# Mamba block and four expert layers on one core: the residual and the norm of a chunk moved from VectorE to TensorE and ScalarE, and both ends of the expert stage put in another order

## The chip, the cores and the metric

The kernel runs on one core of a Trainium2 chip. The metric is the time of one execution on the device, in microseconds (us). A core has five engines with queues of their own: TensorE (PE; its weight loads are shown as PEld), VectorE (DVE), ScalarE (ACT), GpSimd (POOL) and SyncE (SP), which here only issues DMAs.

## The reference

Input x has 4 sequences of 1024 tokens with 128 features. First comes a selective scan block, with 256 inner channels and 64 states each:

```
xn = layernorm(x); xi, z = split(xn @ W_in)
u = silu(causal_conv4(xi) + conv_b);  dt_r, Bm, Cm = split(u @ W_xproj)
delta = softplus(dt_r @ W_dt + b_dt)
h_t = h_{t-1} * exp(delta_t * A) + (delta_t * u_t) * B_t;  y_t = sum_n h_t * C_t
out = ((y + u * D) * silu(z)) @ W_out
x1 = layernorm(x + (x + out))
```

So the scan block's result is `2 x + out`, normalized (mean and variance, no weights). Then come 4 expert layers: a router picks 2 of 4 experts for each token, each expert normalizes its input, multiplies by w1 (128 x 512), takes the gelu and multiplies by w2 (512 x 128); the layer gives the weighted sum of `x + y_e`. The end is `layernorm(x1 + layers(x1))`.

## The kernel before, in words

**Front.** Eight items of 512 tokens are projected, convolved and split in bfloat16 parts, which go through DRAM. This part isn't changed.

**Scan stage.** Tokens are taken in chunks: 64 steps of a pair of sequences, 128 rows in all, 32 chunks (`NCH`). A chunk is two blocks of 128 channels (`kk` 0 and 1), a block eight quarters `q`; quarters 0 to 3 and 4 to 7 make its two groups. `run_blocks` runs `emit(c, pair, kk, last)` over all blocks on every engine, and the numbers `Q_...` say in which quarter an engine does a step for an older chunk. In a quarter

- TensorE computes products for B (`products`, L1180), a part of the sum over states (`sum_states`, L1197) and the arguments of exp for two quarters on (`arguments`, L1167);
- ScalarE computes the exponential for the next scan (`exponent`, L951) and copies products out of PSUM (`take_products`, L961);
- VectorE does one scan instruction of 128 x 1040 (L1519). The first scan of a group waits for all four copies of its group (`evac_done`).

A chunk's output follows two chunks later: ScalarE evacuates y (`evacuate`, L972), TensorE turns it and adds `u * D` (`turn`, L1209, L1211), VectorE gates it (`gate`, L1473), TensorE projects it (`project`, L1219), in block 0, quarter 3. Then VectorE adds the residual (`add_residual`, L1481: `2 x + projection`, into `xres`), takes the statistics (`chunk_stats`, `chunk_aggregate`, L1487, L1493) in quarters 4 to 6 of block 0, GpSimd computes `(var + eps) ** -0.5` (`chunk_rsqrt`, L697, L699), and VectorE writes the normalized rows to `x1c` in quarter 2 of block 1 (`chunk_norm`, L1368). ScalarE's queue stores them. SP loads x's rows, u and silu(z) of the next chunk (`load_post`) once that norm is done.

**Expert stage.** `run_layers` runs `step` for 4 layers x 8 groups of 512 tokens (`n` counts groups through all layers). In a step TensorE does for each expert `first` (L1294, 12 products) and `second` (L1306, 16), in the order first 0, first 1, second 0, transposes of the next group (`stage_xh`, L1273), first 2, second 1, first 3, second 2, second 3. ScalarE does the gelus (L1062, four an expert) and, ahead of expert 2 (in the first step ahead of expert 1, and again ahead of 2), centring and scaling for a group two on (`stage_norm`, L1037, L1043). VectorE has `stage_moments` for the group two on, `start_sum` (L1661), `add_expert` 0 to 3 (L1671), `split_xh` (L1679, L1681: the transposed tile in two parts), `stage_scores` (L1605 on), `stage_router` (L1617 to L1644), `sum_bias` (L1651, L1654). GpSimd computes the router's products (`stage_scores`, L826), the exponential (`stage_exp`, L818), the weighted biases (`stage_bias`, L835) and each `rsqrt` (L688). In the last layer VectorE also finishes the group before (`finish`: `X + X1` L1697, moments L1355 to L1363, scaling L1584), and SP stores it. `begin` holds what an engine does between the last scan and the first step.

A wait is a number that a semaphore has to reach; each engine works through its queue in order. The order is written by hand.

## Time and profile before

| | |
|---|---|
| median of 3 runs | 2242.97 us (2242.24 to 2248.36) |
| the profiled execution | 2246.93 us |
| its span, first to last instruction | 2245.1 us |
| TensorE busy | 2130.0 us (95%) |
| VectorE busy | 1838.6 us (82%) |
| ScalarE busy | 1596.8 us (71%) |
| GpSimd busy | 920.4 us (41%) |
| mean granted TensorE clock | 0.98 of full speed |

Times in the rows are us from the span's start. A row of the timeline has the start, the length, the engine, the line of the kernel, the operation, its output and inputs, and how many instructions were merged in it (x4); in brackets how long the engine had been idle before it, and whose work ended the idle time. Lengths of neighbours overlap: an instruction can start before the one ahead has ended. Scans run from 171.4 to 1355 us, the expert stage from there to the end.

### The profile page before, as it was taken

To read this page: it belongs to the slowest core of one execution; us is meant where nothing else is said; L and a number is where in the kernel's file an instruction comes from. 1 tells how busy PE (TensorE), PEld (TensorE's weight loads), DVE (VectorE), ACT (ScalarE), POOL (GpSimd) and SP (SyncE) were. 2 spreads that over 40 slices of the span, in tenths; PEclk is the share of its full clock that TensorE was granted. 3 is DMA by queue.
4 is the path that set the end of the run, shared out by engine and by line. 5 is a ranking of instruction groups with operands and counts; after the bars stand their busy time and mean duration, and the time that the engine had idled before them with its cause. 6 is when DMAs were issued, how large, how long until landed. Compare 5 with 4: busy or idle time off the path is not lost. (4 is left out here: it accounts for less than half of the span.)

```text
span 2245.1 us, 50361 instructions
## 1 busy us (share of the span) xinstructions
PE 2130.0 (95%) x16960; PEld 1258.0 (56%) x16960; DVE 1838.6 (82%) x2779; ACT 1596.8 (71%) x2070; POOL 920.4 (41%) x452
## 2 busy tenths in 40 slices
PE   7968999999999999999999997999999999999997
PEld 3432333333333333333333335999999999999986
DVE  6869999999999999999999996566555566556665
ACT  5868888888888888888888883545455455445543
POOL 3123334343443444343434344444444444444442
PEclk9977999999999999999999998999999999999999
DMA  5995222222222121212121234000100010000000
GB/s 171 279 281 136 43 46 45 42 46 41 45 42 46 41 46 40 46 40 46 40 46 40 47 96 135 1 0 0 38 1 0 0 39 1 0 1 1 10 11 18
DMA packets 354957, 114.93 MB, mean 51 GB/s; under 512 B 283000, under 2 KB 345600, under 8 KB 354624
## 3 DMA queue, kind: packets, MB, share of 16 engines
q1 hardware_dynamic: 350416, 110.92, 20.2%
q10 hardware_dynamic: 4464, 3.02, 0.4%
...
## 5 line engine op out<-in xcount | busy, mean ns | idle before, releaser
L1519 DVE TENSOR_TENSOR_SCAN arena<-behind 128x1040 f32<-128x1040 f32 x512 | 1157.0, 2309 | 21.1 <-ACT behind L961 18.2
L1062 ACT ACTIVATE arena<-PS,arena 128x512 f32<-128x512 f32 x512 | 342.9, 688 | 399.5 <-PE PS L1294 398.9
L951 ACT ACTIVATE behind<-PS 128x1024 f32<-128x1024 f32 x512 | 526.7, 1029 | 133.9 <-DVE arena L1519 101.3
L1197 PE MATMUL PS<-arena 128*32 128x128 f32 x8192 | 565.9, 406 | 0.0
L961 ACT ACTIVATE behind<-PS 128x1024 f32<-128x1024 f32 x512 | 539.4, 1053 | 20.0 <-PE PS L1180 16.3
L1306 PEld LDWEIGHTS PS<-arena 128*128 128x128 f32 x4096 | 475.8, 193 | 8.1
L1306 PE MATMUL PS<-arena 128*128 128x128 f32 x4096 | 475.9, 276 | 0.0
L771 POOL COPY behind<-carry 128x64 f32<-128x64 f32 x128 | 206.1, 1611 | 518.1 <-DVE arena L1519 384.2
L1294 PE MATMUL PS<-parts_xh,parts_w 128*128 128x512 f32 x1536 | 385.4, 402 | 14.7 <-ACT arena L1062 14.7
L1197 PEld LDWEIGHTS PS<-arena 128*32 128x32 f32 x8192 | 234.6, 119 | 288.1 <-issue 210.9
L1180 PE MATMUL PS<-arena 96*128 96x512 bf16 x1024 | 314.3, 389 | 66.5 <-ACT behind L961 34.6
L1671 DVE SCALAR_TENSOR_TENSOR arena<-PS,arena 128x128 f32 (+1 forms) x512 | 144.0, 344 | 259.8 <-PE PS L1306 258.0
L1294 PEld LDWEIGHTS PS<-parts_xh,parts_w 128*128 128x128 f32 x1536 | 283.9, 191 | 75.6 <-ACT arena L1062 21.1
L1167 PE MATMUL PS<-arena,Ast 96*128 96x512 bf16 x1024 | 314.1, 389 | 3.5 <-ACT behind L951 3.4
L1180 PEld LDWEIGHTS PS<-arena 96*128 96x128 bf16 x1024 | 67.2, 98 | 278.8 <-ACT behind L961 248.6
L1167 PEld LDWEIGHTS PS<-arena,Ast 96*128 96x128 bf16 x1024 | 58.8, 98 | 229.8 <-ACT behind L951 197.6
L818 POOL TENSOR_TENSOR arena<-euler,arena 128x16 f32<-128x16 f32 x32 | 92.6, 2894 | 172.0 <-DVE arena L1612 171.8
L826 POOL TENSOR_TENSOR arena<-arena 128x2048 f32<-128x2048 f32 x32 | 145.6, 4549 | 12.3 <-POOL arena L688 12.3
L835 POOL TENSOR_TENSOR arena<-arena 128x2048 f32<-128x2048 f32 x32 | 115.6, 3612 | 78.3 <-DVE arena L1642 78.3
L688 POOL TENSOR_TENSOR arena<-arena,neg_half 128x4 f32<-128x4 f32 x49 | 50.8, 1037 | 235.3 <-DVE arena L1363 235.3
L785 POOL COPY arena<-arena 64x64 f32<-64x64 f32 x64 | 130.3, 2035 | 11.8 <-POOL behind L771 9.7
L697 POOL TENSOR_SCALAR arena<-arena 128x1 f32<-128x1 f32 x32 | 60.2, 1882 | 160.3 <-DVE arena L1493 160.3
...
## 6 DMA issues: line engine op xcount, KB each, us to landing
...
arena<-dl_d SPq DMA_DIRECT2D x512, 24.0 KB
...
arena<-du_d SPq DMA_DIRECT2D x512, 24.0 KB
...
```

The source lines that it names most:

```text
L771: nc.gpsimd.tensor_copy(seg(dB[:, G_])[:, :, 0], carry[:, pair, d:d + GD]).then_inc(slot_ready, 1)
L826: nc.gpsimd.tensor_tensor(scored, X[:, bass.ds(g * GT, GT), :].unsqueeze(2).broadcast_to([P, GT, E, H]), rw_s[:, bass.ds(l, 1)].broadcast_ ...
L951: nc.scalar.activation(seg(dA[:, half])[:, :, 1:], PS[:, 0:2, :].rearrange("p j (i t) -> p (j i) t", t=TC), ACT.Exp).then_inc(exp_done, 1)
L961: nc.scalar.activation(seg(dB[:, G_])[:, :, 1 + 2 * OCT * r:1 + 2 * OCT * (r + 1)], PS[:, 2:4, :].rearrange("p o (t d) -> p d (o t)", d=GD ...
L1062: nc.scalar.activation(hT[:, e % 2, c], PS[:, HIDDEN[(GT * e + c) % 3], :], ACT.Gelu, bias=bias1[:, lp, e * GT + c:e * GT + c + 1]).then_i ...
L1167: last = nc.tensor.matmul(PS[:, j, :], Ast[0:ROWS, kk * (DB // GI) + 2 * q + j, :], rhs_d[kk][0:ROWS, 2 * q + j].rearrange("r i t -> r (i ...
L1180: last = nc.tensor.matmul(PS[:, 2 + oct_ % 2, :], Bst[kk][0:ROWS, oct_, :], rhs_u[kk][0:ROWS, oct_, :, G_ * GD:(G_ + 1) * GD], start=True, ...
L1197: last = nc.tensor.matmul(PS[32 * j:32 * j + 32, 4 + kk, 0:DB], cd[:, pair, j, 32 * i:32 * i + 32], seg(hb[kk])[:, :, 1 + 16 * j + i], sta ...
L1294: last = nc.tensor.matmul(PS[:, HIDDEN[(GT * e + c) % 3], :], w1p[:, lp, part_w, e, c * P:(c + 1) * P], xhT[:, gp, part_x], start=(part_w ...
L1306: last = nc.tensor.matmul(PS[:, Y_BANK[e], s * P:(s + 1) * P], hT[:, e % 2, c, s * P:(s + 1) * P], w2_s[lp][:, e * GT + c], start=(c == 0) ...
L1519: nc.vector.tensor_tensor_scan(hb[kk][:, q * QD * SEG:(q + 1) * QD * SEG], dA[:, q % 2], dB[:, G_, lo:lo + QD * SEG], 0.0, ALU.mult, ALU.a ...
L1671: last = nc.vector.scalar_tensor_tensor(at(X, g, s), PS[:, Y_BANK[e], s * P:(s + 1) * P], comb[:, gp, s * E + e:s * E + e + 1], at(X, g, s ...
```

## The change

In the scan stage, for all chunks but the last two (`in_end`):

- the residual: `project` adds two products of the identity with `xres` to the same PSUM region, so that it holds `2 x + out`. `add_residual` is gone from VectorE, which takes the statistics straight from PSUM, in quarter 5;
- the norm: ScalarE computes minus the mean (`negate_mean`, quarter 0 of block 1), `x1c = PSUM - mean` (`centre`, quarter 2) and `x1c * rs` (`chunk_norm`, quarter 4); the store moves to quarter 5. `project` and `chunk_aggregate` wait for the norm of the chunk before (`post_done`);
- SP asks for the next chunk's rows after the projection (`out_ready`), no more after the norm.

In the expert stage:

- at its start ScalarE does `stage_norm(0)` ahead of the last evacuation and of b2's load; in the first step the norm of group 1 comes ahead of expert 2, that of group 2 ahead of expert 3; TensorE transposes group 1 after `first` 3, and VectorE splits it after `stage_router`;
- in the last layer `finish` is cut into `finish_moments`, after expert 0's add, and `finish_norm`, after expert 1's; GpSimd's `rsqrt` for it comes between scores and exponential;
- the last group is finished in two halves of two tiles (`finish_half`), the first when `second` 3 has done two of its four tiles (`y_first`; the other two go to PSUM bank 5); SP stores the last group's tiles as the halves come.

```diff
-        Q_EVACUATE, Q_TURN, Q_GATE, Q_PROJECT, Q_SUM, Q_STATS, Q_AGGREGATE, Q_NORM, Q_STORE, Q_CARRY = \
-            1, 6, 7, 3, 4, 5, 6, 2, 3, 3
+        Q_EVACUATE, Q_TURN, Q_GATE, Q_PROJECT, Q_STATS, Q_AGGREGATE, Q_NEGATE, Q_CENTRE, Q_NORM, Q_STORE, Q_CARRY = \
+            1, 6, 7, 3, 5, 6, 0, 2, 4, 5, 3
...
                     if held(chunk - 1):
-                        sp.wait_ge(post_done, chunk - 1)
+                        sp.wait_ge(out_ready, chunk - 1)
...
+                if isinstance(layer[0], int) and layer[0] == NL - 1 and not (isinstance(g, int) and g == 0):
+                    rsqrt(rs_o, o_var, o_rs, g)
                 if more:
                     stage_exp(n + 1)
                     stage_bias(n + 1, new[0] if new else layer[0], 1 - gp)
-                if isinstance(layer[0], int) and layer[0] == NL - 1 and not (isinstance(g, int) and g == 0):
-
-                    rsqrt(rs_o, o_var, o_rs, g)
...
+            def negate_mean(m):
+
+                act.wait_ge(p_var, m + 1)
+                apart(act)
+                nc.scalar.activation(nm_m[:], mv_m[:, 0, 0:1], ACT.Identity, scale=-1.0).then_inc(p_neg, 1)
+
+            def centre(m):
+
+                if held(m):
+                    act.wait_ge(x1_out, 16 * m)
+                act.wait_ge(p_neg, m + 1)
+                apart(act)
+                nc.scalar.activation(x1c, projected(m), ACT.Identity, bias=nm_m[:]).then_inc(p_centred, 1)
+
+            def chunk_norm(m):
+
+                act.wait_ge(p_centred, m + 1)
+                act.wait_ge(p_rs, m + 1)
+                apart(act)
+                nc.scalar.activation(x1c, x1c, ACT.Identity, scale=rs_m).then_inc(post_done, 1)
...
-                    if isinstance(n, int) and n == 0 and e == 1:
+                    begins = isinstance(n, int) and n == 0
+                    if begins and e == 2:
                         stage_norm(1, 1, 1)
-                    if more and e == 2:
+                    if more and e == (3 if begins else 2):
                         stage_norm(n + 2, (g + 2) % NG, gp)
...
-            run_layers(act, lambda first_layer: stage_norm(0, 0, 0), step)
+            def begin(first_layer):
+                stage_norm(0, 0, 0)
+                evacuate(NC - 1, BP - 1, 1)
+                act.dma_start(b2_s, b2.rearrange("p (l e h) -> p l e h", l=NL, e=E)).then_inc(b2_in, 16)
...
                 pe.wait_ge(g_done, m + 1)
+                if held(m) and not (isinstance(m, int) and m == NCH - 1):
+                    pe.wait_ge(post_done, m)
                 for h in range(HALVES):
-                    last = nc.tensor.matmul(projected(m), G[:, h], wout_s[:, h], start=(h == 0), stop=(h == 1))
+                    last = nc.tensor.matmul(projected(m), G[:, h], wout_s[:, h], start=(h == 0),
+                                            stop=(h == 1 and in_end(m)))
+                if not in_end(m):
+                    for r in range(2):
+                        last = nc.tensor.matmul(projected(m), ident_s[:], xres, start=False, stop=(r == 1))
                 last.then_inc(out_ready, 1)
...
                     if kk == 0 and held(chunk - 1):
-                        if q == Q_SUM:
-                            add_residual(chunk - 2)
...
-                    if q == Q_NORM and kk == 1 and held(chunk - 1):
-                        chunk_norm(chunk - 2)
...
+            def finish_half(half):
...
+                for s in range(lo, hi):
+                    last = nc.vector.scalar_tensor_tensor(at(X, g, s), PS[:, y_bank(n, E - 1, s), s * P:(s + 1) * P],
+                                                          comb[:, 1, s * E + E - 1:s * E + E], at(X, g, s),
+                                                          ALU.mult, ALU.add)
...
+                nc.vector.tensor_tensor(xsum_o[:, lo:hi], tiles(X), tiles(X1), ALU.add).then_inc(f_fl, 1)
...
+            finish_half(0)
+            finish_half(1)
+            finish_half_norm(0)
+            finish_half_norm(1)
```

How instructions move, at three places. ScalarE in the scan loop, from the evacuation in quarter 1 of block 1 to the start of quarter 4 (`arena` is the one big buffer in SBUF, `behind` the one for dA and dB). Before:

```order
L972 ACTIVATE arena<-PS 128x128 [waits y_done]
L950 REGISTER_ALU [waits scan_done]
L951 ACTIVATE behind<-PS 128x16x64 [waits arg_ready]
L960 REGISTER_ALU
L961 ACTIVATE behind<-PS 128x64x16 [waits dbp]
L950 REGISTER_ALU [waits scan_done]
L951 ACTIVATE behind<-PS 128x16x64 [waits arg_ready]
L960 REGISTER_ALU
L961 ACTIVATE behind<-PS 128x64x16 [waits dbp]
L978 ACTIVATE carry<-arena 128x128 [waits scan_done]
```

The same stretch now:

```order
L992 ACTIVATE arena<-PS 128x128 [waits y_done]
L970 REGISTER_ALU [waits scan_done]
L971 ACTIVATE behind<-PS 128x16x64 [waits arg_ready]
L980 REGISTER_ALU
L981 ACTIVATE behind<-PS 128x64x16 [waits dbp]
L1010 ISA
L1013 ACTIVATE arena<-PS,nm_m 128x128 [waits x1_out,p_neg]
L970 REGISTER_ALU [waits scan_done]
L971 ACTIVATE behind<-PS 128x16x64 [waits arg_ready]
L980 REGISTER_ALU
L981 ACTIVATE behind<-PS 128x64x16 [waits dbp]
L998 ACTIVATE carry<-arena 128x128 [waits scan_done]
```

The centring (L1013) stands between the copy of quarter 2 and the exponent of quarter 3.

TensorE from the last sums of the scans through the first step of the expert stage. Before:

```order
L1197 MATMUL PS<-arena 32x128 x48
L1273 MATMUL PS<-ident_s,arena 128x128 x4
...
L1294 MATMUL PS<-parts_xh,parts_w 128x512 x12
L1219 MATMUL PS<-wout_s,arena 128x128 x2
L1294 MATMUL PS<-parts_xh,parts_w 128x512 x12
L1306 MATMUL PS<-arena 128x128 x16
L1273 MATMUL PS<-ident_s,arena 128x128 x4
L1294 MATMUL PS<-parts_xh,parts_w 128x512 x12
L1306 MATMUL PS<-arena 128x128 x16
L1294 MATMUL PS<-parts_xh,parts_w 128x512 x12
L1306 MATMUL PS<-arena 128x128 x32
```

And now:

```order
L1352 MATMUL PS<-parts_xh,parts_w 128x512 x12
L1273 MATMUL PS<-wout_s,arena 128x128 x2
L1352 MATMUL PS<-parts_xh,parts_w 128x512 x12
L1364 MATMUL PS<-arena 128x128 x16
L1352 MATMUL PS<-parts_xh,parts_w 128x512 x12
L1364 MATMUL PS<-arena 128x128 x16
L1352 MATMUL PS<-parts_xh,parts_w 128x512 x12
L1331 MATMUL PS<-ident_s,arena 128x128 x4
L1364 MATMUL PS<-arena 128x128 x32
```

Group 1's four transposes moved from behind `second` 0 to behind `first` 3.

VectorE in the loop of the last layer. Before, the finish of the group before stood at the step's end:

```order
L1654 TENSOR_TENSOR arena<-arena 128x512
L1697 ISA
L1697 TENSOR_TENSOR arena<-arena 128x512
L1698 ISA
L1700 ISA
L1355 BN_STATS arena<-arena 128x6 x4
L1357 REGISTER_ALU
L1360 BN_AGGR arena<-arena 128x2 x4
L1362 REGISTER_ALU
L1363 TENSOR_SCALAR arena<-arena 128x4
L1584 SCALAR_TENSOR_TENSOR arena<-arena 128x128 x4
```

Now its first part stands ahead of the split and the reduction of scores:

```order
L1762 TENSOR_TENSOR arena<-arena 128x512
L1763 ISA
L1418 BN_STATS arena<-arena 128x6 x4
L1420 REGISTER_ALU
L1423 BN_AGGR arena<-arena 128x2 x4
L1425 REGISTER_ALU
L1426 TENSOR_SCALAR arena<-arena 128x4
L1743 REGISTER_ALU
L1744 CAST parts_xh<-PS 128x512
L1746 TENSOR_TENSOR parts_xh<-PS,parts_xh 128x512
L1670 TENSOR_REDUCE arena<-arena 128x16
```

The scaling (now L1649) follows expert 1's add.

## Rows read from the trace of the kernel before

**Rows 1.** Windows, one in the scans, one in the experts; busy us by engine.

```profile
600.00:700.00 100.00, 96.51 (x906) 34.57 (x908) 99.91 (x59) 88.65 (x99) 41.45 (x22) 1.00 0.20 42
1700.00:1800.00 100.00, 100.00 (x694) 91.99 (x693) 58.23 (x196) 51.44 (x94) 42.75 (x16) 0.98 0.00 0
```

(The columns: the stretch, its length, then PE, PEld, DVE, ACT and POOL, the granted clock, the DMA engines' share and GB/s.)

**Rows 2.** Timeline of VectorE, one chunk of the scans.

```profile
701.13 2.32 DVE L1519 TENSOR_TENSOR_SCAN arena<-behind 128x1040 f32<-128x1040 f32 x1
...
703.55 2.32 DVE L1519 TENSOR_TENSOR_SCAN arena<-behind 128x1040 f32<-128x1040 f32 x1
...
710.59 2.32 DVE L1519 TENSOR_TENSOR_SCAN arena<-behind 128x1040 f32<-128x1040 f32 x1
...
715.04 2.30 DVE L1519 TENSOR_TENSOR_SCAN arena<-behind 128x1040 f32<-128x1040 f32 x1
...
717.50 11.18 DVE L1519 TENSOR_TENSOR_SCAN arena<-behind 128x1040 f32<-128x1040 f32 x5
```

**Rows 3.** Timeline of ScalarE, same chunk.

```profile
709.32 1.05 ACT L961 ACTIVATE behind<-PS 128x1024 f32<-128x1024 f32 x1
...
714.88 0.28 ACT L972 ACTIVATE arena<-PS 128x128 f32<-128x128 f32 x1
715.24 1.03 ACT L951 ACTIVATE behind<-PS 128x1024 f32<-128x1024 f32 x1
...
717.45 1.03 ACT L951 ACTIVATE behind<-PS 128x1024 f32<-128x1024 f32 x1 [0.24 <-DVE arena L1519]
...
718.38 1.05 ACT L961 ACTIVATE behind<-PS 128x1024 f32<-128x1024 f32 x1
```

**Rows 4.** Timeline of TensorE, same chunk, at the projection.

```profile
700.87 0.61 PE L1219 MATMUL PS<-wout_s,arena 128*128 128x128 f32 x4
701.32 0.60 PE L1180 MATMUL PS<-arena 96*128 96x512 bf16 x2
...
702.88 0.61 PE L1167 MATMUL PS<-arena,Ast 96*128 96x512 bf16 x2
...
704.89 0.61 PE L1167 MATMUL PS<-arena,Ast 96*128 96x512 bf16 x2
```

**Rows 5.** Timelines of TensorE, GpSimd and VectorE, start of the expert stage.

```profile
1367.45 1.08 PE L1273 MATMUL PS<-ident_s,arena 128*128 128x128 f32 x4 [3.22 <-ACT arena L1043]
...
1395.11 1.65 PE L1294 MATMUL PS<-parts_xh,parts_w 128*128 128x512 f32 x3 [5.78 <-ACT arena L1062]
...
1412.11 3.21 PE L1294 MATMUL PS<-parts_xh,parts_w 128*128 128x512 f32 x13
...
1364.22 4.51 POOL L826 TENSOR_TENSOR arena<-arena 128x2048 f32<-128x2048 f32 x1
...
1371.27 2.28 DVE L1605 TENSOR_REDUCE arena<-arena 128x16 f32<-128x2048 f32 x1
...
1394.69 0.69 DVE L1681 TENSOR_TENSOR parts_xh<-PS,parts_xh 128x512 fp32r<-128x512 f32 x1
...
1406.00 0.17 DVE L1644 TENSOR_REDUCE arena<-arena 128x4 f32<-128x16 f32 x1
```

**Rows 6.** Waits of TensorE, from 2000 us on: total, times, longest.

```profile
PE PS L1294 <- ACT arena L1062: 4.3, 4, 1.3
```

**Rows 7.** Timelines of GpSimd and VectorE, early in the scans.

```profile
178.03 4.07 POOL L733 TENSOR_TENSOR arena<-arena 128x2048 bf16<-128x2048 f32 x1 [10.30 <-ACT arena L904]
...
179.83 4.45 DVE L1519 TENSOR_TENSOR_SCAN arena<-behind 128x1040 f32<-128x1040 f32 x1 [1.59 <-ACT behind L951]
```

**Rows 8.** Timelines of TensorE, VectorE and SP, end of the program.

```profile
2225.13 7.30 PE L1306 MATMUL PS<-arena 128*128 128x128 f32 x64
...
2234.44 1.12 DVE L1671 SCALAR_TENSOR_TENSOR arena<-PS,arena 128x128 f32<-128x128 f32 x4
...
2239.10 1.14 DVE L1584 SCALAR_TENSOR_TENSOR arena<-arena 128x128 f32<-128x128 f32 x4 [1.12 <-POOL arena L688]
...
2241.99 1.28 SPq L669 DMA_DIRECT2D out_dram<-arena  x2
```

102 lines of the change are left out of this document (83 added, 19 removed).

## The prediction

> **What bounds the kernel now.** I read the windows first. In a window of the scan stage VectorE is busy 99.9 of 100 us, TensorE 96.5 and ScalarE 88.7; in a window of the expert stage TensorE is busy all the time and the others about half [rows 1]. So an edit in the scans counts by what it takes from VectorE's path, an edit in the experts by TensorE's idle time at the seam between the stages, in the last layer and behind its last product. Then I took single instructions of one chunk (two blocks of 8 scans) apart.
>
> Back to back, scans start every 2.22 us: (11.18 - 2.30) / 4 [rows 2]. Two places of the chunk are longer because of operations that the change takes away: the gap with the residual sum, 701.13 to 703.55, is 2.42, and the one with the norm, 715.04 to 717.50, is 2.46 [rows 2]. So they cost 0.20 and 0.24 us, less than their durations, since neighbours overlap. VectorE's full claim is 0.44 us a chunk, 30 chunks, **13.2 us**.
>
> But ScalarE and TensorE stand close behind. ScalarE's exponent starts about when the scan before the current one ends, the copy of products 0.93 later (717.45, 718.38), and lasts 1.05; after it an extra operation takes 0.36 (714.88 to 715.24) [rows 3]. At the 4th and the 8th scan of a block that copy must be done before the next scan may start. At 709.32 + 1.05 = 710.37 the copy ends, at 710.59 the scan behind it starts [rows 2, 3]: there ScalarE's chain, not VectorE, sets the time.
>
> **Scans, the norm.** Taken from VectorE: 0.24. Now the third scan of block 1 is followed at once by the fourth, at 717.26; ScalarE can't begin its exponent before 717.45 (the scan's end), its copy ends at 719.43, and the scan that needs it can start some 0.12 later, at 719.55, where it was 717.50 + 2.23 = 719.73 [rows 2, 3]. So **0.17 us** of the 0.24 are left. The three operations added to ScalarE (negate, centre, norm, 0.36 each) fall in quarters 0, 2 and 4 of block 1; with the two that are there already, each of quarters 0 to 4 holds one: 0.92 + 0.94 + 0.36 = 2.22, just the scan's 2.22, so they cost nothing, with no margin. If they cost 0.1 us more each, the three before the 4th copy make it 0.3 late.
>
> **Scans, the residual.** Taken from VectorE: 0.20. Added to TensorE: two products with the identity, which the projection's two price: 0.45 (700.87 to 701.32) [rows 4]. Their results come no later than needed; what is late is the chain of argument products behind. TensorE needs 2.01 us a quarter (702.88 to 704.89) and has 2.22, so it regains 0.2 a quarter [rows 4]. Walked forward from 701.32 with 0.45 more: arguments at 703.33, 705.34, 707.63 (this one after waiting for a copy), exponent 708.32, copy to 710.30, scan at 710.52 against 710.59 [rows 2, 3, 4]. So **0.07 us** of 0.20 reaches the end of the block. Bounds: nothing, if the products cost 0.1 more; 0.20, if TensorE's rows hide slack. The statistics read PSUM now instead of SBUF; any change lies beside that late chain, so it costs nothing.
>
> Together 0.24 x 30 = **7.2 us** (0 to 13.2, and a small loss if ScalarE's lack of margin bites). Asking for the next chunk's rows at the projection gains nothing: the transfer wasn't waited for, VectorE's window has no idle time [rows 1]. SP asks some 8 us earlier, and its 5 requests go before the next block's loads, for which it still waits.
>
> **Seam.** TensorE waited 3.22 us for the first centred tile, because ScalarE evacuated the last sums first [rows 5]. With the norm first, transposes and split are 3.2 us earlier. What follows is led by another chain: GpSimd's scoring, 1364.22 + 4.51 = 1368.73, is not moved; VectorE's reduction stood at 1371.27 and can come after a norm and a small copy that the running scoring holds up, at 1369.4 [rows 5]. So the chain is 1.9 to 3.2 us earlier; I take 2.6, as the last projection isn't late any more. The weights of group 1 then end at 1406.17 - 2.6 = 1403.6 [rows 5]. The split of group 1 comes now behind them, twice 0.69: 1405.0 [rows 5]. On TensorE, experts 1 and 3 no longer wait for group 1's norm, but the last expert waits for group 2's, 2.6 earlier than the break at 1395.11; 17.0 us of work followed up to 1412.11 [rows 5], of which two products' worth of work (6.3 by the same rows at full clock) lies ahead now: ready at about 1403.7. Group 1 starts at 1405.1 where it started at 1412.11: **7.0 us** (3 to 9).
>
> **Last layer.** TensorE stalls there 4 times, 4.3 us in all, waiting for ScalarE's gelu [rows 6]. This comes from VectorE, which finishes the group before (4.7 us: from the end of the add at 2235.56 to the norm's end at 2240.24 [rows 8]) ahead of expert 3's add. The change cuts that in two and puts it where VectorE waits for GpSimd. It looks like 4.3 us gained. Against it: the first operation there adds two tensors in SBUF while GpSimd scores, and a scan that started 1.8 us into a GpSimd operation of 4.07 us took 4.45 instead of 2.30: it stood until 182.10, where GpSimd ended [rows 7]. If the add is held in the same way, it starts only when the scoring ends, and the 2.5 us of moments (4.7 less norm and rsqrt wait, 1.14 and 1.12 [rows 8]) and the split (1.4) stand in front of the reduction: 3.9 later. The norm reads two tensors too, is held by the exponential that runs then, and adds its own 1.1. 3.9 + 1.1 - 4.7 = 0.3 us more per group, not less. I take **1 us lost** over six groups (4.3 gained to 2 lost).
>
> The Trainium skill says in "SBUF — State Buffer", section "Who interferes with whom", that a VectorE instruction with two SBUF inputs contends with a GpSimd instruction that reads SBUF, and that the later one is fully blocked. My row shows this for a scan only; the page extends it to the plain addition. Without it the sum is the one of the first rival.
>
> **End.** TensorE ends at 2225.13 + 7.30 = 2232.43, the last norm at 2240.24, 7.8 later, 2.0 of it since the group before was still being finished [rows 8]. Now the first half (two tiles) is done while TensorE computes the second. Behind its end stand: two adds 0.6, add 0.4 and perhaps 0.4 held by GpSimd's rsqrt, moments 1.2, rsqrt with the half before in its way 1.8, norm 0.6: 5.0, so 2.8 less. Of four requests, 0.73 apart (1.28 - 0.55), two are left behind the last norm: 1.4 less [rows 8]. **4.2 us**.
>
> **Sum.** -7.2 - 7.0 + 1.0 - 4.2 = -17.4 us. The profiled execution took 2246.93 us (span 2245.1), 4.0 over the median of 2242.97; so 2229.5 against the first, and **2225.5** as a median.
>
> **Rivals.**
> - The last layer's add isn't held (GpSimd frees it in time): 4.3 us gained instead of 1 lost, 2220. For it: adds that read PSUM run beside the scoring unhindered. Against: the scan of [rows 7]. Chance 0.17.
> - VectorE's whole 0.44 us counts, since exponents catch up through slack that start times hide: 6 us more, 2219.5. Chance 0.13.
> - ScalarE becomes the bound of block 1: 0.3 us late at the fourth copy, so no gain and 0.06 lost a chunk: 9 us fewer, 2234.5. For it: 2.22 against 2.22. Chance 0.12.
> - The seam brings only 2 us: TensorE's half clock after its new break before the last expert, or a GpSimd operation between, is longer than my walk has it: 2230.5. Chance 0.08.
> - The change does nothing that can be measured, if two of these meet: 2242. Chance 0.04.
> - **Slower**: the residual products don't overlap as the projection's do and cost their recorded length, 0.61 a group and more. Everything beyond 0.45 goes straight into the late chain and the scan at 710.59, 30 times. It decides from 1.25 us for both (17.4 + 6.7 lost over 30 chunks); at 1.4 us the time is 2254. Against it: TensorE runs at full clock there [rows 1]. Chance 0.04.
>
> **Numbers.** My forecast holds 0.42, its own range 2220 to 2230. 0.3% is 6.7 us, about what a measurement of this kernel can tell from no change; the three runs lie 6.1 apart. All cases but the last two and a quarter of ScalarE's are faster by more: 0.90 faster, 0.06 same, 0.04 slower. The range takes in the first three rivals and the fourth: 2212 (the first two together reach 2214) to 2235.
>
> **What would show it.** Right: chunks 0.24 us closer to each other; the fifth scan of a block still waiting for ScalarE's copy; from the last product of the scans' sums to group 1's first product 7 us less than before; in the last layer an addition of about 4 us instead of 0.68, and stalls of TensorE still there; a last norm 5 us after TensorE's end. Wrong: chunks closer by 0.44, or not at all; an addition of 0.68 beside a running scoring; TensorE idle between its experts in the first group by more than 8 us.

## The result, and the profile after

The changed kernel takes **2208.47 us** (2207.10 to 2209.82, 5 runs) where the kernel before took 2242.97 (2240.86 to 2248.36, 5 runs beside it): a ratio of 0.9838, 95% interval 0.9827 to 0.9849, or 34.5 us less. The forecast was 2225.5, its range 2212 to 2235: the direction is right, the gain is twice what was forecast, and below the range. The profiled execution took 2209.82 us, with a span of 2208.2: 36.9 less than the span before.

I cut both traces at the same events. The first cut is the first gate of a chunk (VectorE's product ahead of the projection), the second the start of the last scan, the third TensorE's first product of group 1, the fourth the first product of the last step.

| stretch | before, us | after, us | gain | forecast |
|---|---|---|---|---|
| start to the first gate | 249.2 | 240.7 | 8.6 | 0 |
| to the last scan | 1103.5 | 1094.0 | 9.5 | 7.2 |
| to group 1's first product | 59.4 | 51.2 | 8.2 | 7.0 |
| to the last step | 794.9 | 789.3 | 5.5 | -1.0 |
| to the end of the span | 38.1 | 33.1 | 5.1 | 4.2 |

Of the 19.5 us that the sum is off in the span, 8.6 lie in a stretch whose code the change doesn't touch, and 6.5 in the stretch with the last layer. The rows follow in the order of the stages.

**Front.** The row of the DMA view, 60 to 160 us, first before and then after: packets, megabytes, mean rate. The DMA engines are busy nearly all the time in both (shares of 0.99 and 1.00).

```profile
DMA packets 50733, 28.65 MB, mean 286 GB/s; under 512 B 22759, under 2 KB 47335, under 8 KB 50727
```

```profile
DMA packets 53209, 30.32 MB, mean 303 GB/s; under 512 B 22867, under 2 KB 49747, under 8 KB 53203
```

Over these 100 us the transfers run 6% faster. The first scan, which waits for them, starts at 163.4 instead of 171.4 us.

**Scans.** The windows that answer to [rows 1]:

```profile
600.00:700.00 100.00, 98.12 (x927) 36.84 (x926) 99.78 (x56) 90.48 (x105) 41.21 (x22) 1.00 0.20 42
1700.00:1800.00 100.00, 100.00 (x694) 92.02 (x693) 59.66 (x199) 51.20 (x94) 43.10 (x15) 0.98 0.07 22
```

TensorE has 1.6 us more in 100, ScalarE 1.8; VectorE is idle for 0.2. Its timeline over one chunk, for [rows 2]: the fifth scan of block 0 (the one at 701.13 there), the first of block 1 (710.59 there), the fifth of block 1, and the first of the next chunk, behind the gate.

```profile
688.76 2.33 DVE L1588 TENSOR_TENSOR_SCAN arena<-behind 128x1040 f32<-128x1040 f32 x1
...
698.06 2.32 DVE L1588 TENSOR_TENSOR_SCAN arena<-behind 128x1040 f32<-128x1040 f32 x1
...
707.02 2.32 DVE L1588 TENSOR_TENSOR_SCAN arena<-behind 128x1040 f32<-128x1040 f32 x1
...
716.32 2.32 DVE L1588 TENSOR_TENSOR_SCAN arena<-behind 128x1040 f32<-128x1040 f32 x1
```

From the fifth scan of block 0 to the first of block 1, where the residual was, it is 9.30 us where it was 9.46. From there to the scan behind the gate it is 18.26 where it was 18.42: 710.59 in [rows 2] and, in the kernel before,

```profile
729.01 11.29 DVE L1519 TENSOR_TENSOR_SCAN arena<-behind 128x1040 f32<-128x1040 f32 x5
```

ScalarE and TensorE in the same chunk, for [rows 3] and [rows 4]:

```profile
695.85 1.03 ACT L971 ACTIVATE behind<-PS 128x1024 f32<-128x1024 f32 x1 [0.26 <-PE PS L1219]
...
699.96 0.20 ACT L1005 ACTIVATE nm_m<-arena 128x1 f32<-128x1 f32 x1
...
704.56 0.36 ACT L1013 ACTIVATE arena<-PS,nm_m 128x128 f32<-128x128 f32 x1
...
708.99 0.40 ACT L1020 ACTIVATE arena<-arena 128x128 f32<-128x128 f32 x1
```

```profile
688.94 0.61 PE L1277 MATMUL PS<-arena,ident_s 128*128 128x128 f32 x4
...
690.96 0.61 PE L1219 MATMUL PS<-arena,Ast 96*128 96x512 bf16 x2
...
692.97 0.61 PE L1219 MATMUL PS<-arena,Ast 96*128 96x512 bf16 x2
...
695.21 0.60 PE L1219 MATMUL PS<-arena,Ast 96*128 96x512 bf16 x2
```

The chain that the prediction walked is there: late arguments, an exponential that waits for them (`[0.26 <-PE]`), a copy, and the first scan of block 1 behind that copy.

**Start of the expert stage**, for [rows 5]: TensorE, then ScalarE and VectorE.

```profile
1373.31 1.65 PE L1352 MATMUL PS<-parts_xh,parts_w 128*128 128x512 f32 x3 [5.73 <-ACT arena L1109]
...
1385.82 7.39 PE L1352 MATMUL PS<-parts_xh,parts_w 128*128 128x512 f32 x24 [2.35 <-DVE parts_xh L1746]
```

```profile
1370.10 1.28 ACT L1083 ACTIVATE arena<-arena 128x128 f32<-128x128 f32 x4 [7.42 <-DVE arena L1660]
```

```profile
1363.07 3.45 DVE L1639 COPY arena<-arena 128x128 f32<-128x128 f32 x1
```

TensorE's wait ahead of the last expert is still there, only earlier. It waits for gelus that are queued behind group 2's norm, and that norm waits 7.42 us for VectorE's moments. Ahead of these moments in VectorE's queue stands a copy of 128 x 128: it takes 3.45 us, where the same copy at 1350.51 took 0.23, and it ends just behind GpSimd's product of 1362.73 to 1366.43.

**Last layer.** Where [rows 6] had TensorE waiting 4.3 us, there is no wait of TensorE left. The addition of one group beside GpSimd's scoring, and the norm of the next beside the exponential:

```profile
2105.02 4.57 POOL L846 TENSOR_TENSOR arena<-arena 128x2048 f32<-128x2048 f32 x1 [0.43 <-POOL arena L708]
...
2108.53 1.62 DVE L1762 TENSOR_TENSOR arena<-arena 128x512 f32 x1
```

```profile
2142.03 2.89 POOL L838 TENSOR_TENSOR arena<-euler,arena 128x16 f32<-128x16 f32 x1 [3.15 <-DVE arena L1677]
```

```profile
2143.07 1.13 DVE L1649 SCALAR_TENSOR_TENSOR arena<-arena 128x128 f32<-128x128 f32 x4
```

**End**, for [rows 8]: TensorE's last products, VectorE's adds of the second half, the last norm.

```profile
2193.30 7.30 PE L1364 MATMUL PS<-arena 128*128 128x128 f32 x64
```

```profile
2201.05 0.60 DVE L1786 SCALAR_TENSOR_TENSOR arena<-PS,arena 128x128 f32<-128x128 f32 x2
...
2204.08 0.61 DVE L1649 SCALAR_TENSOR_TENSOR arena<-arena 128x128 f32<-128x128 f32 x2 [0.33 <-POOL arena L708]
```

TensorE ends at 2200.60, the last norm at 2204.69: 4.09 later, where it was 7.81.

A caution on the profiled stretch of the experts: the granted clock of TensorE falls to half (1.2 GHz) for a few us there now and then, and the stretch from group 1's first product to the last step goes by how long. Six profiles have the old code in it (the one before and the five runs below that only move tensors in it). They take 791.7 us with 6.8 us of the stretch at half clock, 793.3 to 793.4 with 10.2 (four of them), and 794.9 with 13.7. Nine profiles have the changed code: 786.3 with 6.8 (three), 787.9 to 788.0 with 10.2 (four), 789.3 and 789.5 with 13.7. So two kernels are compared at the same time at half clock, and the change is worth 5.4 to 5.6 us there at each of the three. The stretch of the scans repeats within 0.3 us.

### The profile page after: what moved, and what is told of

The parts are those of the page before. It is cut to its first block, busy times and chain, and to the rows that moved or that the text cites. A ratio compares the mean times of both kernels' runs of the same rounds, so it can differ in the third digit from the quotient of the medians.

```text
span 2208.2 us, 50669 instructions
## 1 busy us (share of the span) xinstructions
PE 2133.7 (97%) x17080; PEld 1270.6 (58%) x17080; DVE 1833.8 (83%) x2721; ACT 1617.4 (73%) x2160; POOL 926.1 (42%) x453
## 4 chain that ended last, share of the span: by engine, by line
PE 41%; DVE 29%; issue 23%; SPq 3%; ACT 2%; POOL 1%; DVEq 1%; DMA 0%; ACTq 0%; POOLq 0%
DVE arena L1588 25%; PE PS L1364 20%; PE PS L1352 16%; PE PS L1249 1%; ACT behind L981 1%; SPq L519 1%; SPq L615 1%; SPq L521 1%; PE PS L1232 1%; ACT behind L971 1%; PE PS L1331 1%; PE PS L1219 1%; PE PS L1340 1%; DVE arena L1431 0%; PE PS L1142 0%
## 5 line engine op out<-in xcount | busy, mean ns | idle before, releaser
L791 POOL COPY behind<-carry 128x64 f32<-128x64 f32 x128 | 212.9, 1664 | 508.2 <-ACT carry L998 266.8
L1352 PEld LDWEIGHTS PS<-parts_xh,parts_w 128*128 128x128 f32 x1536 | 284.2, 191 | 68.5 <-ACT arena L1109 10.3
L838 POOL TENSOR_TENSOR arena<-euler,arena 128x16 f32<-128x16 f32 x32 | 92.6, 2895 | 166.1 <-DVE arena L1677 165.9
L708 POOL TENSOR_TENSOR arena<-arena,neg_half 128x4 f32<-128x4 f32 (+1 forms) x50 | 50.7, 1014 | 226.7 <-DVE arena L1426 226.6
```

The lines of the kernel that those rows point to most:

```text
L791: nc.gpsimd.tensor_copy(seg(dB[:, G_])[:, :, 0], carry[:, pair, d:d + GD]).then_inc(slot_ready, 1)
L1352: last = nc.tensor.matmul(PS[:, HIDDEN[(GT * e + c) % 3], :], w1p[:, lp, part_w, e, c * P:(c + 1) * P], xhT[:, gp, part_x], start=(part_w ...
```

## The experiments

Each was timed against the kernel before, in 4 to 11 runs. Where a stretch is named it is one of the table above.

### The front: where the large tensor begins

The change adds a one-column tensor `nm_m` ahead of `arena`, which moves `arena` (and what lies behind it) by 32 bytes in SBUF. The kernel before, with an unused column:

```diff
+        pad = sb("pad", [P, 1])
         arena = sb("arena", [P, ARENA])
```

> The kernel before with one unused column in SBUF ahead of the arena, nothing else. It moves the arena from byte 29664 of a partition to byte 29696 (as the change does with its new column for the negated mean), so the large transfers of the front read and write addresses that are whole multiples of 64 bytes. Theory 'address': the front ends some 8 us earlier (first scan near 163.4 us instead of 171.4, DMA near 300 to 310 GB/s instead of 269 to 302 between 60 and 140 us), time ratio about 0.9965 (2235 us). Rival 'change of code': the 8 us come from somewhere in the change's instructions, or from one profiled run differing from another: first scan near 171.4, ratio 1.000.

**Measured:** 2236.35 us, ratio 0.9958 (0.9945 to 0.9972), first scan at 162.7. An unused column of four bytes makes this kernel 0.4% faster, and all of the front's gain is there.

```profile
DMA packets 53240, 30.28 MB, mean 303 GB/s; under 512 B 22898, under 2 KB 49778, under 8 KB 53234
```

The other way round, the changed kernel with `nm_m` allocated behind everything:

```diff
-        nm_m = sb("nm_m", [P, 1])
         ...
         spare = sb("spare", [P, BEHIND - 2 * 2 * E * F - 2 * 2 * GT * P])
+        nm_m = sb("nm_m", [P, 1])
```

> The changed kernel with its new column for the negated mean allocated behind everything else, so that the arena is back at byte 29664. Theory 'address': first scan back at about 171.4 us (163.4 in the changed kernel), ratio to the kernel before 0.9838 + 0.0036 = 0.9874 (2214.7 us). Rival 'change of code': first scan stays at 163.4, ratio 0.984.

**Measured:** 2218.53 us, ratio 0.9876 (0.9861 to 0.9891), first scan at 173.2, 286 GB/s. The gain of the front is gone, the rest is kept.

Which multiple does it take? A pad of nine columns, or the one-column constant `euler` moved behind, or more constants (`...` stands for lines left out):

```diff
+        pad = sb("pad", [P, 9])
```

> The kernel before with nine unused columns ahead of the arena: the arena moves by 64 bytes to byte 29728, which again leaves a remainder of 32 when divided by 64. Theory 'address by remainder': first scan near 171.4 us as before, ratio 1.000. Rival 'any shift helps' (other neighbours in SBUF, a layout effect of another kind): first scan near 163.4, ratio 0.9965.

```diff
-        euler = sb("euler", [P, 1])
         ...
+        euler = sb("euler", [P, 1])
```

> The kernel before with the one-column constant moved from ahead of the arena to behind everything: the arena begins at byte 29632, a multiple of 64 but of no higher power than 128 down to 64 (29696 in the change is a multiple of 512). Theory 'a multiple of 64 is enough': first scan near 163.4 us, ratio 0.9965. Rival 'it takes a multiple of 512': first scan near 171.4, ratio 1.000, or something between.

```diff
-        rb_s = sb("rb_s", [P, NL * E])
...
-        neg_half = sb("neg_half", [P, 4])
-        euler = sb("euler", [P, 1])
+        pad = sb("pad", [P, 1])
...
+        neg_half = sb("neg_half", [P, 4])
+        euler = sb("euler", [P, 1])
+        rb_s = sb("rb_s", [P, NL * E])
```

> The kernel before with three small constants moved behind everything else and one unused column: the arena begins at byte 29568, a multiple of 128 and not of 256. Known so far, by the time of the first scan: 29664 (multiple of 32) 171.4 us, 29728 (32) 171.7, 29632 (64) 170.3, 29696 (512) 162.7. Theory 'the larger the power of two, the better, in steps': between 170.3 and 162.7, some 167 us, ratio 0.998. Theory 'only a multiple of 512 counts' (row pieces of 512 bytes in the large transfers): about 170, ratio 0.998 to 1.000. Theory '128 is enough': 163, ratio 0.996.

```diff
-        rb_s = sb("rb_s", [P, NL * E])
-        g_s = sb("g_s", [P, NL * E])
-        lb_s = sb("lb_s", [P, NL * E])
...
```

and the rest as in the edit before, all five behind everything.

> The kernel before with five small constants moved behind everything else and one unused column: the arena begins at byte 29440, a multiple of 256 and not of 512. Theory 'in steps': 165 us to the first scan. Theory 'only a multiple of 512': about 170, ratio 0.998 to 1.000. Theory '256 is enough': 163, ratio 0.996.

**Measured**, with the runs above in their place:

| arena begins at byte | a multiple of | first scan, us | GB/s, 60 to 160 us | ratio to before |
|---|---|---|---|---|
| 29664 (before) | 32 | 171.4 | 286 | 1 |
| 29728 (9 columns) | 32 | 171.7 | 287 | 0.9987 (0.9978 to 0.9996) |
| 29632 (`euler`) | 64 | 170.3 | 288 | 0.9984 (0.9975 to 0.9993) |
| 29568 | 128 | 170.1 | 286 | 0.9985 (0.9976 to 0.9994) |
| 29440 | 256 | 163.5 | 303 | 0.9966 (0.9953 to 0.9979) |
| 29696 (1 column) | 512 | 162.7 | 303 | 0.9958 (0.9945 to 0.9972) |

It is a step between 128 and 256, not the one at 64 that I had expected, nor a slope. The first scan is 7 to 9 us earlier, and the median of the whole kernel 5 to 7 below those of the three shifts that don't help. (Those three lie some 0.15% under the kernel before, which the traces don't explain.) The front also varies by itself: of the profiles with `arena` at 29696 one, of a version further down (`e17_late_norm`), has its first scan at 167.3, with 300 GB/s, and the others at 162.7 to 164.2.

The Trainium skill has, in "DMA: Bandwidth & Descriptors", section "How a descriptor splits into AXI transactions", that a transaction must start at a multiple of 256 bytes, so that a descriptor which doesn't begin at one starts its first transaction at the boundary below and pays for the unused bytes too. A step at 256 agrees with that. But by the Trainium skill's rule the unused bytes would grow with the distance from the boundary. For transfers that begin a multiple of 256 bytes into `arena` this distance is 224, 32, 192 and 128 bytes in the first four rows, and the rates there are 286, 287, 288 and 286 GB/s: the traces show no such growth.

It is `arena` that counts. `behind` begins 158016 bytes after it, 64 more than a multiple of 256, so that in the run with `euler` moved it is `behind` that lies on a multiple of 256 (187648), and the front doesn't gain. Which of `arena`'s transfers gain, the runs don't tell.

### The scans

The residual back on VectorE:

```diff
+                        if q == 4:
+                            add_residual(chunk - 2)
...
-                if not in_end(m):
-                    for r in range(2):
-                        last = nc.tensor.matmul(projected(m), ident_s[:], xres, ...)
...
-                        sp.wait_ge(out_ready, chunk - 1)
+                        sp.wait_ge(post_done, chunk - 1)
```

(The statistics and ScalarE's centring read the sum in SBUF then.)

> The changed kernel with the residual back on VectorE (sum in quarter 4, statistics and centring read its result in SBUF; the two products with the identity left out; the next rows asked for when the norm is done, since the sum now reads and writes them until then). The prediction's theory: 0.07 us a chunk, so 2.1 us longer. What the trace shows at the end of the block (9.30 instead of 9.46): 0.16 a chunk, 4.8 us longer, 2213. Rival 'VectorE's whole 0.20 counts': 6.0 us. Rival 'the products cost more than they free': faster than the changed kernel. Chunk period 36.53 now; 36.60, 36.69 or 36.73 then.

**Measured:** 2239.24 us, ratio 0.9975 (0.9965 to 0.9985); the scans' stretch 1123.6 us instead of 1094.0. No theory had this. Its timelines, TensorE at the turn of a chunk and VectorE behind the gate:

```profile
615.31 0.49 PE L1261 MATMUL PS<-arena,diag_s 128*128 128x128 f32 x2 [0.59 <-DMA arena<-in_x]
```

```profile
618.30 11.34 DVE L1581 TENSOR_TENSOR_SCAN arena<-behind 128x1040 f32<-128x1040 f32 x5 [0.87 <-ACT behind L981]
```

TensorE waits for the rows of x, VectorE for a copy behind that. So I suspected the last part of the edit, SP's wait. To see it alone, the changed kernel with SP's wait only:

```diff
-                        sp.wait_ge(out_ready, chunk - 1)
+                        sp.wait_ge(post_done, chunk - 1)
```

> The changed kernel with one wait of SP changed back: the next chunk's rows are asked for when the chunk's norm is done, not at its projection. The prediction costed this part of the change at nothing, since no transfer was waited for: 2208.5 us, chunk period 36.53. The theory after the run with the residual on VectorE (2239.2 us, TensorE waits 1.2 us for the rows ahead of each turn, ScalarE's copy and a scan behind it 0.9 late): with the norm on ScalarE two quarters and more later than on VectorE, rows asked for behind it come too late for the turn in quarter 6: a VectorE gap of 0.8 to 0.95 us in each chunk, 25 to 28 us in all, 2234 to 2237 us.

**Measured:** 2236.02 us, ratio 0.9962 (0.9950 to 0.9973); scans 1122.5 us. SP's queue, VectorE and the waits from 600 to 700 us:

```profile
608.80 0.96 SPq L570 DMA_DIRECT2D arena<-u_d  x2
609.85 1.04 SPq L570 DMA_DIRECT2D arena<-sz_d  x2
611.10 0.57 SPq L572 DMA_DIRECT2D arena<-in_x  x1
```

```profile
616.36 13.57 DVE L1588 TENSOR_TENSOR_SCAN arena<-behind 128x1040 f32<-128x1040 f32 x6 [0.86 <-ACT behind L981]
```

```profile
PEld PS L1261 <- DMA arena<-in_x: 3.3, 3, 1.2
```

The rows are asked for from 608.8 to 611.7 and TensorE wants them at about 612.8; the last of them land at 613.34, and its first product of the turn starts at 613.39. In the kernel before they land 3.9 us ahead of the turn (611.66, 615.53), in the changed kernel 10.3 (703.20, 713.50). Earlier asking, which I had costed at nothing, holds 28.5 us of this kernel. By these 3.9 us it gains nothing over the kernel before, where the norm came early, though no run shows it alone there; but without it the norm on ScalarE, two quarters later and more, costs far more than it gains.

Then the residual alone, with the rows asked for once ScalarE has centred the chunk:

```diff
-                        sp.wait_ge(post_done, chunk - 1)
+                        sp.wait_ge(p_centred, chunk - 1)
```

> The kernel with the residual back on VectorE once more, now with the next rows asked for as soon as ScalarE has centred the chunk (the last read of the sum), some 4.4 us earlier than at its norm. If the loss of the run before it was the late rows and nothing else, TensorE doesn't wait for them and the cost of the residual alone shows: 0.07 us a chunk by the prediction (2210.6 us), 0.16 by the end of the block in the two traces (2213.3, period 36.69), 0.20 if VectorE's whole claim counts (2214.5). Rival 'something else in that version is slow': 2239 again.

**Measured:** 2212.35 us, ratio 0.9856 (0.9840 to 0.9872); scans 1098.7, so 4.7 us for the residual, 0.16 a chunk. (The interval of the ratio reaches that of the changed kernel; the stretch, which repeats within 0.3 us, tells them apart.) And the norm alone, back on VectorE, with ScalarE's three operations left out:

```diff
-                        if q == Q_NORM:
-                            chunk_norm(chunk - 2)
...
+                    if q == 2 and kk == 1 and held(chunk - 1):
+                        chunk_norm(chunk - 2)
```

> The changed kernel with the chunk's norm back on VectorE (one subtract and multiply in quarter 2 of block 1, reading the projection's bank; ScalarE's three operations left out). The prediction's theory: 0.17 us a chunk come back, period 36.53 to 36.70 us, 30 chunks 5.1 us, time 2213.6. Rival 'VectorE's whole claim': 0.24 a chunk, 2215.7. Rival 'ScalarE's three operations cost something': less than 0.17 a chunk, down to nothing. The norm is done about one block quarter pair earlier than on ScalarE, the next rows are asked for at the projection as in the changed kernel.

**Measured:** 2216.91 us, ratio 0.9878 (0.9861 to 0.9894); scans 1100.7, so 6.7 us for the norm, 0.22 a chunk. The four corners of this square, in us of the scans' stretch: neither 1103.5, norm only 1098.7, residual only 1100.7, both 1094.0. Alone, the norm gains 4.8 (0.16 a chunk) and the residual 2.8 (0.09): together 1.9 more than the sum. A row of the corner with the residual only tells why:

```profile
708.70 0.39 DVE L1425 TENSOR_SCALAR arena<-PS,arena 128x128 f32<-128x128 f32 x1
```

With the residual on TensorE a norm on VectorE has to read the bank in PSUM. It lasts 0.39 us where it was 0.32 reading SBUF, and from the first to the fifth scan of the block around it it is 9.21 us (702.03 to 711.24) instead of 9.14: 0.07 a chunk, 30 chunks, 2.1 us.

### The start of the expert stage

ScalarE's old order alone:

```diff
-                stage_norm(0, 0, 0)
                 evacuate(NC - 1, BP - 1, 1)
                 act.dma_start(b2_s, ...)
+                stage_norm(0, 0, 0)
```

> The changed kernel with ScalarE's start of the expert stage back in its old order (last sums evacuated, bias load asked for, then the first group's norm). The prediction's theory: the chain through scoring and reduction is 1.9 to 3.2 us later, so group 1 starts 2.6 us later: from the last scan's start to group 1's first product 53.8 us instead of 51.2, time 2211 us. Rival: the start is led by GpSimd's scoring alone, whose place this does not move: nothing, 51.2 and 2208.5 us. Second rival: TensorE's half clock behind the longer break adds one or two us more: 55 to 56.

**Measured:** 2211.34 us, ratio 0.9848 (0.9831 to 0.9864); the stretch to group 1 54.5 us, 3.3 more.

Group 1's norm, transposes and split in their old places alone, and with them group 2's norm, ahead of expert 2 again:

```diff
-                    if begins and e == 2:
+                    if begins and e == 1:
                         stage_norm(1, 1, 1)
-                    if more and e == (3 if begins else 2):
+                    if more and e == 2:
...
-                if more and not begins:
+                if more:
                     stage_xh(n + 1, 1 - gp)
...
-                if begins:
-                    stage_xh(1, 1)
...
-                    if not begins:
-                        split_xh(n + 1, 1 - gp)
+                    split_xh(n + 1, 1 - gp)
...
-                if begins:
-                    split_xh(1, 1)
```

> The changed kernel with group 1's norm, its transposes and its split back in their old places in the first step (ahead of expert 1's gelus, behind expert 0's second product, ahead of the reduction of the scores). By the prediction's walk group 1 then starts only when the last expert has waited for group 2's norm as before: 7.0 - 2.6 = 4.4 us later; with the 8.2 us that the trace shows for the whole seam, 5.6 later: from the last scan's start to group 1's first product 55.6 to 56.8 us, time 2213 to 2214. Rival: the earlier norm alone brings the gain, and this order is worth nothing: 51.2 and 2208.5.

**Measured:** 2212.67 us, ratio 0.9854 (0.9836 to 0.9873); 54.7 us, 3.5 more. Undone one at a time the two cost 6.7 us, undone both (the kernel before) 8.2. The intervals of both ratios reach that of the changed kernel (0.9827 to 0.9849), so the whole time doesn't tell these 3 us by itself; the stretches do. Behind them the experts take 786.3 us in both, as the changed code does with 6.8 us at half clock, so nothing is given back there. The half clock explains little of the seam: in the old code's six profiles this stretch takes 58.2 to 59.4 us with 10.2 to 17.1 at half clock, in the changed kernel 51.2 with 6.8.

Now forward, against the wait that is left: group 2's norm behind the last expert's gelus in the first step, and group 1's split back ahead of the reduction, where VectorE waits.

```diff
-                    if more and e == (3 if begins else 2):
+                    if more and e == 2 and not begins:
                         stage_norm(n + 2, (g + 2) % NG, gp)
                     ...
+                if begins:
+                    stage_norm(2, 2, 0)
...
-                    if not begins:
-                        split_xh(n + 1, 1 - gp)
+                    split_xh(n + 1, 1 - gp)
...
-                if begins:
-                    split_xh(1, 1)
```

> A version meant to beat the changed kernel: in the first step ScalarE's norm of group 2 stands behind the last expert's gelus, not ahead of them (it waits 7.4 us for VectorE's moments, and TensorE waits 5.7 us for the gelus behind it), and VectorE's split of group 1 stands back ahead of the reduction of the scores, in the 3.7 us in which VectorE waits for GpSimd. Walk: TensorE's 5.7 us of idle time before expert 3's last products and the 2.35 before group 1 go, as does the half clock behind them (about 1.5): group 1's first product at 1376.5 to 1378 instead of 1385.8, from the last scan's start 42 to 43.5 us instead of 51.2, time 2199 to 2201 us. Rival: group 1's expert products then wait for the router's weights of group 1 (ready at 1384.2) or for GpSimd's bias products (1387.8), and half of it is given back: 2204.

**Measured:** 2210.02 us, ratio 0.9842 (0.9829 to 0.9855): no better than the changed kernel. Group 1 did start 10.2 us earlier in its stretch (41.0 for 51.2), and then TensorE stood, here with ScalarE's row:

```profile
1396.32 1.65 PE L1354 MATMUL PS<-parts_xh,parts_w 128*128 128x512 f32 x3 [8.31 <-ACT arena L1109]
```

```profile
1393.11 1.28 ACT L1083 ACTIVATE arena<-arena 128x128 f32 x4 [10.45 <-DVE arena L1662]
```

It is the same wait one group later: gelus queued behind a norm that waits for VectorE's moments. So the norm has to stand behind the gelus in every step (the edit against the version just shown):

```diff
-                    if more and e == 2 and not begins:
-                        stage_norm(n + 2, (g + 2) % NG, gp)
...
-                if begins:
-                    stage_norm(2, 2, 0)
+                if more:
+                    stage_norm(n + 2, (g + 2) % NG, gp)
```

> The reordered version (e13) with ScalarE's norm of the group after next behind the last expert's gelus in every step, not in the first alone. There the 10.2 us gained by group 1's start were given back: in group 1 ScalarE waited 10.45 us for VectorE's moments with the last expert's gelus queued behind it, and TensorE stood for 8.3. Walk: that stall goes, group 2 starts 8.3 us earlier, later groups may wait a little while VectorE and GpSimd (some 23.5 us of chained work a group against TensorE's 25.7) catch up. Expected 2199.5 to 2202 us, ratio to the kernel before 0.980. Rival: the lateness of VectorE and GpSimd (moments of group 3 at 1391.3) is the real bound and TensorE waits for the split or for expert weights a step later: 2206 or more.

**Measured:** 2200.94 us, ratio 0.9802 (0.9786 to 0.9819). With VectorE's moments of group 2 pulled ahead as well:

```diff
                 stage_router(0, 0)
+                stage_moments(2, 2)
                 chunk_norm(NCH - 1)
...
-                if more:
+                begins = isinstance(n, int) and n == 0
+                if more and not begins:
                     stage_moments(n + 2, (g + 2) % NG)
```

> The same, with VectorE's moments of group 2 right behind group 0's router instead of behind the copy and the bias sum (which GpSimd's running product holds up for 3.5 us anyway). GpSimd's next scoring starts at 1368.3 instead of 1371.4, so the whole chain of group 1 is 3.1 us earlier and what stalls are left in groups 1 and 2 go too: 2198 to 2200 us, ratio 0.9795, if those stalls exist; the same as the version without it, if they don't.

**Measured:** 2199.85 us, ratio 0.9802 (0.9788 to 0.9815). The waits of TensorE from 1340 to 1460 us that are left in this version:

```profile
PE PS L1352 <- DVE parts_xh L1746: 1.7, 2, 1.1
PE PS L1352 <- ACT arena L1107: 0.8, 1, 0.8
```

This version beats both kernels, the changed one by 8 us (0.9802 against 0.9838). The share of the last edit can't be told from nothing: without it group 1 starts 41.0 us after the last scan, with it 42.3.

### The last layer

The finish of the group before in its old place, on VectorE and GpSimd:

```diff
                 add_expert(n, g, gp, 0)
-                    finish_moments(g - 1)
...
                 add_expert(n, g, gp, 1)
-                    finish_norm(g - 1, 1 - gp)
...
                     sum_bias(n + 1)
+                    finish_moments(g - 1)
+                    finish_norm(g - 1, 1 - gp)
```

> The changed kernel with the last layer's finish back in its old place (VectorE: whole, ahead of expert 3's add; GpSimd: its rsqrt behind the products for the output bias); halves at the end are kept. The prediction's theory (the add held by the scoring and the norm held by the exponential eat the gain, 1 us lost): putting it back makes it 1 us faster, 2207.5 us, TensorE's stalls from 2000 us on some 4.3 us in both. Theory after reading the trace (the hold of the add is real, the norm is not held, VectorE has 2 us to spare, so nothing of it reaches TensorE): stalls of 4.3 to 5.5 us come back and the time is 5 us longer, 2213.5 us, ratio to the kernel before 0.986; the stretch from the first product of group 1 to the start of the last step grows from 789.3 to about 794.9.

**Measured:** 2217.86 us, ratio 0.9873 (0.9857 to 0.9890) against 0.9838, so 7.9 us longer (9.4 by the two medians). TensorE's waits are back (3.8 us in four). The stretch to the last step takes 792.9 us with 10.2 at half clock, 4.9 more than the changed code has with as much. And, which neither theory had, the end is longer too: from TensorE's last product to the end of the span 11.5 us instead of 7.6, as the group before is finished while the last one's first half is ready.

Only the moments moved, behind the reduction:

```diff
                 add_expert(n, g, gp, 0)
-                    finish_moments(g - 1)
...
                     stage_scores(n + 1, next_l)
+                    finish_moments(g - 1)
```

> The changed kernel with one call moved: in the last layer the moments of the group before stand behind the reduction of the scores, no longer ahead of the split. If the addition's 1.62 to 2.26 us come from GpSimd's scoring beside it, it takes 0.68 us in all six groups now, VectorE's loop in that stretch falls by 1 to 1.5 us from 26.0 us a group or its idle time ahead of expert 0's add grows by as much, and the scores reach GpSimd's exponential about 3.4 us earlier. The total: no change (2208.5), since TensorE doesn't wait there in the changed kernel. Rival 'the addition is long for another reason': 1.6 to 2.3 us there too.

**Measured:** 2210.31 us, ratio 0.9847 (0.9832 to 0.9862). The addition in the changed kernel, then in this one: least, median and most ns of seven.

```profile
L1762 DVE TENSOR_TENSOR arena<-arena x7: 680/1315/2256, 2031.5 to 2185.5; 128x512 f32 x6, 128x512 f32<-128x512 f32 x1
```

```profile
L1762 DVE TENSOR_TENSOR arena<-arena x7: 682/693/694, 2033.8 to 2184.6; 128x512 f32 x6, 128x512 f32<-128x512 f32 x1
```

Away from the scoring, all seven take 0.69 us, so the scoring is what made them long. VectorE's busy time from 2050 to 2176 us falls from 92.6 to 88.5, but its loop gets longer, not shorter: the moments of the group two on come every 26.3 to 26.5 us instead of 26.0. GpSimd's queue has the `rsqrt` of the finish ahead of the exponential, and now that waits for the late moments (scores ready at 2112.86, exponential at 2116.51; in the changed kernel 2141.95 and 2142.03). So the expected earlier exponential didn't come, and TensorE's last two steps take 26.1 and 26.5 us instead of 25.7.

### The end

The last group finished whole, in one bank and stored behind its one norm, the rest as changed:

```diff
-            finish_half(0)
-            finish_half(1)
-            finish_half_norm(0)
-            finish_half_norm(1)
+            finish_moments(NG - 1)
+            finish_norm(NG - 1, 1)
```

> The changed kernel with the last group finished whole (one bank, one add, one rsqrt, one norm), its four rows stored behind the one norm; the rest of the change stays, so nothing of the group before is finished behind expert 2 any more. The prediction has TensorE's end to the last norm 5.0 instead of 5.8 (7.8 less the 2.0 of the group before) and 1.4 for the stores, so 0.8 + 1.4 = 2.2 us for the halves: 2210.7 us; if VectorE waits 1.1 for the held add as before, the same. Rival 'the halves are worth the whole 4.2 or 5.1': 2213. Rival 'the second rsqrt and the shared engines eat it': 2208.5.

**Measured:** 2212.37 us, ratio 0.9854 (0.9838 to 0.9871). From TensorE's end to the span's 10.4 us, between 12.7 before and 7.6 with halves. So the halves are worth 2.8, and moving the finish of the group before 2.3 (3.9 with the halves in place, by the run above). The norm of this version:

```profile
2204.71 1.14 DVE L1646 SCALAR_TENSOR_TENSOR arena<-arena 128x128 f32<-128x128 f32 x4 [1.19 <-POOL arena L708]
```

## Why the prediction fell short

**Front: a term that wasn't there.** This is the step that took the time out of the range. "What bounds the kernel now" began with the scans, and the sum had nothing for 171 us of front, without a reason given; none of its code changes. But the change's one new column moved the arena to a multiple of 256 bytes, and that is worth 8.6 us of span by the trace; the two pairs of ratios say as much (0.9958 against 1 is 9.4 us, 0.9876 against 0.9838 is 8.5). This is the largest single part of the error.

**Last layer: "0.3 us more per group, not less" failed.** The mechanism it rests on is real: the addition is held by the scoring; in six groups in a row it takes 0.68, 0.98, 1.31, 1.62, 1.95 and 2.26 us. Three sizes were off. The walk let it lose nearly the whole scoring; but VectorE waits 2.0 to 3.1 us for TensorE ahead of expert 0's add in the five groups where it is held, and so comes when the scoring is 2.9 to 4.1 us under way, so that only its rest counts (3.5 at 2108.53, and some 0.3 earlier with each group). The walk let the norm be held by the exponential; its four instructions took 1.13 us in all beside it. And it didn't ask whether VectorE had time to lose. From the first to the last of seven groups its moments are 27.35 us apart before and 26.1 after, against TensorE's 25.7: it falls 0.4 us behind a group, no longer 1.65, and in the last of them it still waits 2.0 us for TensorE. So the rival of 2220 was right about the size (4.3 us of waits gone, and 5.5 of time) for another reason: held, and harmless.

**Scans: the norm's walk was right, the residual's 0.09 short.** Where the norm was, from the first to the fifth scan of block 1, it is 8.96 us now (698.06 to 707.02), and the walk gave 719.55 - 710.59 = 8.96; before it was 9.14. Where the residual was, it is 9.30 for 9.46: 0.16 of VectorE's 0.20 arrive, where the walk had 0.07. Together 0.32 a chunk, for 0.24, and 9.5 us for 7.2. The step that was mis-sized is the late chain at its end. Moved by 12.37 us, so that the fifth scans of block 0 coincide, the rows have the arguments at 703.33 and 705.34, as walked, then 707.58 for 707.63, the exponent at 708.22 for 708.32 and the scan at 710.43 for 710.52. That the residual alone gains 0.09, near the forecast, is luck: it is these 0.16 less the 0.07 by which a norm on VectorE gets slower when it reads PSUM. ScalarE's lack of margin did no harm: its operations take 0.20, 0.36 and 0.40 us, and the scan behind the fourth copy (707.02) comes 2.29 us after the one before it, as the walk had it (717.26 to 719.55).

**Asking for the rows: "gains nothing" fits the trace of before and misleads.** The step was costed by itself, against that trace. In the changed kernel it is what keeps 28.5 us from being lost.

**Seam: 7.0 forecast, 8.2 measured.** The part for ScalarE's order was taken as 2.6 between 1.9 and 3.2; by the stretches of the two runs and of before it is 4.7 alone and 3.3 on top of the other. The part for group 1's order was 4.4, and is 4.9 alone and 3.5 on top. They overlap by 1.4, which adding them left out. The break ahead of the last expert came as forecast, and is 5.73 us. (The 1403.7 of the working should be 1403.2 by its own terms, 1395.11 - 2.6 + 17.0 - 6.3; the split at 1405.0 decides either way.)

**End: 4.2 forecast, 5.1 measured.** The stores were given 1.4 and have 1.3 (from the norm's end to the span's 4.9 before, 3.5 after). The last norm was expected to end 5.0 us behind TensorE's end, and it is 4.09. The term that was too large is the second `rsqrt`, 1.8 us "with the half before in its way": from the last moment (2203.24) to the norm it is 0.84. The half before was answered 1.4 us ahead of it, and it takes 0.73 us for two columns, where four took 1.01.

The range failed by the first of these: the changed kernel without the front's gain took 2218.53 us, inside it (2215.2 by its ratio to the kernel before). The forecast itself would still have been 7 to 10 us too long there, by the last layer above all.

## What to carry to other kernels

Before a change is priced, compare the addresses of the tensors that large transfers use: a tensor of four bytes moved one of 158 KB a partition onto a multiple of 256 bytes, and the 8.6 us gained by that are more than the 4.8 to 6.7 that the norm on ScalarE, which it served, is worth in the scans. Price edits that share data or a deadline in pairs, not one by one: an enabling edit shows as nothing when it is costed against the old kernel. Before an operation is called too dear, look for the idle time that it falls into: the held addition cost up to 1.6 us a group and nothing of the time. A wait that is taken away in one step of a pipeline comes back in the next one, unless the order that makes it is changed in all of them.

## What the runs showed of the chip

- Transfers out of and into SBUF, at a DMA share of about 1, ran at 303 GB/s (300 in one profile) with the big tensor's start at a multiple of 256 bytes and 286 to 288 with multiples of 32, 64 and 128.
- A plain addition of two SBUF tensors on VectorE was held while GpSimd ran a product of two SBUF tensors (up to 2.26 us instead of 0.69, and longer by 0.3 with each group as it starts earlier in the product; it ends 0.55 us after the product in all five). With the addition moved away from the product it took 0.69 in all seven groups. The Trainium skill's rule in "SBUF — State Buffer", section "Who interferes with whom", agrees with that. But the norm, whose second SBUF input is one column read 128 times, wasn't held beside GpSimd's exponential of 128 x 16, which reads SBUF too: 1.13 us for four at 2143.07, inside 2142.03 to 2144.92. By the Trainium skill's rule it would wait until 2144.92; the trace disagrees. Which of the two makes the difference wasn't tried.
- VectorE's norm of 128 x 128 takes 0.39 us from PSUM and 0.32 from SBUF.
